# fc1 of a macaron block as seven half-size products (one level of Strassen's scheme) on one Trainium2 core

## What is computed

```python
x = x + 0.5 * ffn(layernorm(x))            # ffn: real(ifft(fft(x) @ w)) + bias, a 512 x 512 product M
x = x + attn(layernorm(x))
x = x + 0.5 * ffn(layernorm(x))
# attn(x):
h = layernorm(x) * norm1_w + norm1_b
x = x + causal_conv(h, K) + D * h          # K = mix @ exp(-tau dt t), per channel
g = layernorm(x) * norm2_w + norm2_b
g = gelu(g @ fc1_w.T + fc1_b)              # 512 -> 2048
g = g @ fc2_w.T + fc2_b                    # 2048 -> 512
return x + g
```

## Time and profile before

| | us |
|---|---|
| median of 3 runs (lowest to highest) | 2140.52 (2140.36 to 2143.08) |
| the profiled execution, its own time | 2143.72 |
| span of the profile | 2141.9 |
| PE busy | 1965.4 |
| DVE busy | 1247.0 |
| ACT busy | 748.8 |
| POOL busy | 537.4 |
| mean granted clock of TensorE | 0.969 of full |

### The profile page before, as it was taken

The page is one execution under the profiler, slowest core; times in us unless marked ns, Lnnn a source line. Parts: engine busy times, 40 slices in busy tenths (PEclk is TensorE's granted clock), DMA queues, the critical chain, the costliest instruction groups (busy, mean ns, idle before and its releaser), DMA issues.

```text
span 2141.9 us, 27911 instructions
## 1 busy us (share of the span) xinstructions
PE 1965.4 (92%) x10107; PEld 963.8 (45%) x10128; DVE 1247.0 (58%) x2099; ACT 748.8 (35%) x1003; POOL 537.4 (25%) x416
## 2 busy tenths in 40 slices
PE   7975877498859999999999999999999999999997
PEld 6432333276634444444444444444444444444443
DVE  4876999777955637274562727446282644628242
ACT  1365777664633314032230413223041322404111
POOL 0165777653421202021120201112020111202101
PEclk8997999799979999999999999999999999999998
DMA  7144332379781122131212213121222212122011
GB/s 246 79 174 160 118 118 98 94 199 311 229 250 40 40 59 58 62 79 36 64 40 59 60 60 78 40 59 40 60 60 64 74 40 59 40 59 60 25 35 40
DMA packets 231288, 191.02 MB, mean 89 GB/s; under 512 B 142594, under 2 KB 176898, under 8 KB 230403
## 3 DMA queue, kind: packets, MB, share of 16 engines
q1 hardware_dynamic: 231172, 189.34, 30.4%
HBM read 100.69 MB, written 63.41 MB: 77 GB/s over the span
## 4 chain that ended last, share of the span: by engine, by line
PE 78%; DVE 7%; DMA 5%; issue 5%; POOL 2%; ACT 2%; SPq 1%; ACTq 0%; DVEq 0%; POOLq 0%; another core or an unknown queue 0%
PE psum L1555 31%; PE psum L1572 31%; PE psum L1459 9%; DMA arena<-in_x 3%; PE psum L1510 2%; PE psum L1501 1%; PE psum L1422 1%; DVE ring L1189 1%; DVE arena L1133 1%; DVE bn L966 1%; DVE bn L1141 1%; PE psum L1519 1%; PE psum L1433 1%; PE psum L1440 1%; DVE taps L1089 1%
## 5 line engine op out<-in xcount | busy, mean ns | idle before, releaser
L1555 PE MATMUL psum<-arena 128*128 128x512 f16 x3072 | 668.6, 380 | 25.1 <-DMA arena<-taps 24.7
L1572 PE MATMUL psum<-arena 128*128 128x512 f16 x3072 | 665.7, 379 | 0.0
L846 ACT ACTIVATE arena<-psum,b1p,sc 128x512 f32<-128x512 f32 x256 | 199.2, 778 | 1060.1 <-PE psum L1555 1059.0
L1555 PEld LDWEIGHTS psum<-arena 128*128 128x128 f16 x3072 | 300.7, 98 | 391.2 <-issue 31.8
L1572 PEld LDWEIGHTS psum<-arena 128*128 128x128 f16 x3072 | 300.5, 98 | 362.5
L565 POOL TENSOR_TENSOR va<-va,mhalf 128x4 f32<-128x4 f32 x80 | 91.0, 1141 | 1249.2 <-DVE va L959 1226.3
L1376 DVE SCALAR_TENSOR_TENSOR arena<-psum,sc,arena 128x512 f32<-128x512 f32 x64 | 48.0, 751 | 578.7 <-PE psum L1572 578.7
L1352 DVE SCALAR_TENSOR_TENSOR arena<-arena,sc 128x512 f16<-128x512 f32 x256 | 243.9, 953 | 9.1
L1459 PE MATMUL psum<-m_parts,taps 128*128 128x512 f16 x768 | 183.6, 390 | 69.5 <-DVE taps L1089 69.1
L1459 PE MATMUL psum<-m_parts,arena 128*128 128x512 f16 x768 | 170.8, 383 | 10.3 <-DMA arena<-taps 10.3
L1349 DVE TENSOR_SCALAR arena<-arena,sc 128x512 f16<-128x512 f32 x256 | 137.6, 537 | 51.1 <-ACT arena L846 50.8
(11 more groups left out here) (159 smaller groups left out, 1767.5 us busy)
## 6 DMA issues: line engine op xcount, KB each, us to landing
arena<-in_x SPq DMA_DIRECT2D x16, 1024.0 KB, 9.8
x_scratch<-arena SPq DMA_DIRECT2D x16, 1024.0 KB, 4.3
...
```

The source lines that it names most:

```text
L846: act.activation(h32[:, hc % 4, :], bank(hc % 2), ACT.Gelu, scale=scale(C_W1), bias=b1p[:, hc:hc + 1])\
L1555: last = pe.matmul(bank(hc % 2), w1_sb[:, a, k, hc * P:(hc + 1) * P], gt[:, b, k, :], start=(n == 0), stop=(n == 3 * KC - 1))
L1572: last = pe.matmul(bank(4 + j % 2), hid[:, a, hc, j * P:(j + 1) * P], w2_sb[:, b, hc, :], start=(n == 0), stop=(n == 3 * HC - 1))
```

## The change

The 2048 x 512 weight matrix is cut into blocks A11, A12, A21, A22 of 1024 hidden rows and 256 inputs, the 512 tokens of a group into two halves (tiles 0, 1 and tiles 2, 3). Seven products of 1024 x 256 by 256 x 256, for the combinations A11, A12, S1, S4, S3, N2, A22 of blocks (PROD = 7), take the place of eight. Per pair p of hidden chunks (HP = 8 pairs) each product is 2 (k) x 3 matmuls of 256 columns. Their sums are formed in three PSUM chains: chain a takes A11, then N2, S3 and A22, and is copied out by ACT after the first three (h_first, h_second, h_third); chain b holds A12; chain c S1, then S4. DVE adds them (c11, c22, c12) in `h32`, ACT takes Gelu there.

With it come: hid_high (the high part of the hidden activation) goes from DVE to POOL; z2 gets three more combinations (z2_mix) and is split and turned in two halves of three DMAs, through one buffer; z3_parts has two buffers for four tiles and the whole z3 stands in the PSUM banks 4 and 5; the second product stands behind step 4 of fc1 rather than behind fc1; mixed, residual and z2 of the next group stand behind fc1; each parity has one buffer for r and x2, so the load of r waits for the store of the output two groups before. In the preparation POOL mixes the scaled blocks (w1_mix), in two parts, the second during the first tiles of the first pass; ACT and DVE split them; the scratch holds 7 MB where it held 4, and 3 MB of it are loaded after the others. The scale of fc1's weights is 4 times lower.

```diff
+PROD = 7
+HB = HID // 2
+HP = HC // 2
+CB = C // 2
+TB = GT * P // 2
...
-        rbuf = [buffer(at4), buffer(at3)]
-        x2buf = [buffer(at3 + size), buffer(at3 + 2 * size)]
...
+        rbuf = [buffer(at2 + 3 * size), buffer(at4 + 2 * gt_cols + size)]
...
+        h32 = [ring[:, 0:2, :], ring[:, 2:4, :], spare[:, 2 * C:4 * C].rearrange("p (i c) -> p i c", i=2)]
+        z3_parts = spare[:, 0:2 * C].bitcast(F16).rearrange("p (j s c) -> p j s c", j=2, s=2)
+        z2_parts = taps_flat[:, 0:PROD * 2 * CB].rearrange("p (n s c) -> p n s c", n=PROD, s=2)
+        z3t = taps_flat[:, 2 * one_block:4 * one_block].rearrange("p (j s k t) -> p j s k t", j=GT, s=2, k=KC)
+        extra = psum[:, 6:8, :].rearrange("p a b -> p (a b)")[:, 0:3 * CB].rearrange("p (n c) -> p n c", n=3)
+        TURNS = ((0, 2), (2, 4), (4, 7))
...
+            def turn_z2(g, half):
+                for i, (a, b) in enumerate(TURNS):
+                    sp.wait_ge(z2_low, 6 * g + 3 * half + i + 1)
+                    sp.sem_inc(gate, 1)
+                    sp.dma_start_transpose(gt[:, 4 * a:4 * b, half * P:(half + 1) * P],
+                                           z2_parts[:, a:b, :, :].rearrange("p n s c -> p (n s c)"))\
+                      .then_inc(gt_turned[i], 16)
...
-                    sp.wait_ge(z2_low, 4 * g + 4)
+                    sp.wait_ge(z2_low, 6 * g + 6)
...
+                    sp.wait_ge(x3_ready, 4 * g)
+                    sp.dma_start(rows(out, g - 1), rbuf[1 - par]).then_inc(out_stored[1 - par], 16)
...
+                    if not is_first(g):
+                        sp.wait_ge(out_stored[1 - par], 16 * (pair + par))
+                    load_r(g + 1, 1 - par)
+                    sp.wait_ge(product[S4], HP * g + HP)
+                    sp.sem_inc(gate, 1)
+                    for half in range(2):
+                        turn_z2(g + 1, half)
...
+            def w1_mix(k):
+                pool.wait_ge(w1_scaled, 4 * k + 4)
+                a22, a21, a11, a12 = [scaled[k][:, i, :] for i in range(4)]
+                pool.tensor_tensor(a22, a21, a22, ALU.add).then_inc(w1_mixed, 1)
+                pool.tensor_tensor(a21, a11, a21, ALU.subtract).then_inc(w1_mixed, 1)
+                pool.wait_ge(w1_mixed, 4 * k + 2)
+                pool.tensor_tensor(a11, a11, a22, ALU.subtract).then_inc(w1_mixed, 1)
+                pool.wait_ge(w1_mixed, 4 * k + 3)
+                pool.tensor_tensor(a12, a12, a11, ALU.add).then_inc(w1_mixed, 1)
...
+            def hid_high(g, p, lower):
+                ready = (h22_ready, h1_ready)[lower]
+                pool.wait_ge(ready, HP * g + p + 1)
+                if not lower:
+                    pool.wait_ge(h21_ready, HP * g + p + 1)
+                if p == 0 and not lower and not is_first(g):
+                    pool.wait_ge(fc2_psum, 4 * g)
+                pool.sem_inc(gate, 1)
+                pool.tensor_scalar(hid[:, 0, p if lower else HP + p, :], h32[p % 3][:, 0 if lower else 1, :],
+                                   scale(S_H), None, ALU.mult).then_inc(h_high, 1)
...
+                for p in range(HP):
+                    hid_high(g, p, False)
+                    hid_high(g, p, True)
+                    if not is_first(g) and p < 4:
+                        x2_biased(g - 1, p, 1 - par)
...
+                for s in range(HP + 1):
+                    p, n = s, HP * g + s + 1
+                    if s < HP:
+                        act.wait_ge(product[A11], n)
+                        if p >= 3:
+                            act.wait_ge(h_low, HC * g + 2 * p - 4)
+                        elif not is_first(g):
+                            act.wait_ge(h_low, HC * g)
+                        act.activation(h32[p % 3][:, 0, low], chain_a(p), ACT.Copy)\
+                           .then_inc(h_first, 1)
+                    if s > 0:
+                        q = s - 1
+                        act.wait_ge(product[S3], n - 1)
+                        act.activation(h32[q % 3][:, 1, high], chain_a(q), ACT.Copy)\
+                           .then_inc(h_third, 1)
+                        if not is_first(g) and s <= 4:
+                            z3_norm(g - 1, 1 - par, s - 1)
+                    if s < HP:
+                        act.wait_ge(product[N2], n)
+                        act.activation(h32[p % 3][:, 0, high], chain_a(p), ACT.Copy)\
+                           .then_inc(h_second, 1)
+                    if s > 0:
+                        act.wait_ge(c22_sum, n - 1)
+                        gelu(g, q, False, high, h32[q % 3][:, 1, high], h22_ready)
+                        act.wait_ge(product[A22], n - 1)
+                        gelu(g, q, False, low, chain_a(q), h21_ready)
+                        act.wait_ge(c12_sum, n - 1)
+                        gelu(g, q, True, whole, h32[q % 3][:, 0, whole], h1_ready)
+                if not is_last(g):
+                    z2_all(g + 1)
...
+            def z2_mix(g, half):
...
+                dve.tensor_tensor(extra[:, 0, :], second[:, 1, :], second[:, 0, :], ALU.subtract)\
+                   .then_inc(z2_mixed, 1)
+                dve.tensor_tensor(second[:, 0, :], second[:, 0, :], first[:, 0, :], ALU.subtract)\
+                   .then_inc(z2_mixed, 1)
+                dve.tensor_tensor(extra[:, 1, :], second[:, 0, :], second[:, 1, :], ALU.subtract)\
+                   .then_inc(z2_mixed, 1)
+                dve.tensor_tensor(extra[:, 2, :], first[:, 1, :], extra[:, 1, :], ALU.add).then_inc(z2_mixed, 1)
...
+            def z3_whole(g, j, par):
+                if j >= 2 or not is_first(g):
+                    dve.wait_ge(z3_low, 4 * g + j - 1 if j >= 2 else 4 * g)
+                dve.tensor_scalar(bank(4 + j % 2), rbuf[par][:, j, :], va[:, 4, j:j + 1], va[:, 5, j:j + 1],
+                                  ALU.mult, ALU.add).then_inc(z3_ready, 1)
...
+                for s in range(HP + 1):
+                    if s > 0:
+                        c22(g, s - 1)
+                    if s > 1:
+                        hid_low(g, s - 2, False)
+                    if s < HP:
+                        c11(g, s)
+                    if not is_first(g) and s < 4:
+                        z3_whole(g - 1, s, 1 - par)
+                    if s > 0:
+                        c12(g, s - 1)
+                    if s > 1:
+                        hid_low(g, s - 2, True)
+                    if not is_first(g) and 1 <= s < 5:
+                        z3_split(g - 1, s - 1)
+                    if not is_first(g) and s == 4:
+                        for j in range(GT):
+                            x3(g - 1, j, 1 - par)
+                hid_low(g, HP - 1, False)
+                hid_low(g, HP - 1, True)
+                if not is_last(g):
                     for j in range(GT):
+                        mixed(g + 1, j, pair + par, 1 - par)
+                    mixed_shift(g + 1)
+                    for j in range(GT):
+                        residual(g + 1, j, 1 - par)
+                x2(g, 0, par)
+                if not is_last(g):
+                    z2_mix(g + 1, 0)
+                    z2_split(g + 1, 0)
+                    z2_mix(g + 1, 1)
+                x2(g, 1, par)
+                if not is_last(g):
+                    z2_split(g + 1, 1)
+                x2(g, 2, par)
+                x2(g, 3, par)
...
-                pe.wait_ge(z3t_turned[j], 16 * (g + 1))
-                if not (is_first(g) and j < 2):
+                pe.wait_ge(z3t_turned[j % 2], 16 * (2 * g + j // 2 + 1))
+                if j == 0:
+                    pe.wait_ge(z3_low, 4 * g + 4)
+                if j >= 2:
                     pe.wait_ge(x3_ready, 4 * g + j - 1)
-                ffn(bank(6 + j % 2), z3t[:, j, :, :, :], ffn2_psum)
-            pe.wait_ge(w1_loaded, 16 * 8)
...
+            def part_product(i, p, chain, start, stop):
+                n = 0
+                for k in range(2):
+                    for a, b in PASSES:
+                        last = pe.matmul(chain(p),
+                                         w1_sb[i][:, a, k, p * P:(p + 1) * P], gt[:, 4 * i + 2 * b + k, :],
+                                         start=start and n == 0, stop=stop and n == 5, skip_group_check=True)
+                        n += 1
+                last.then_inc(product[i], 1)
+            def p1(g, p):
+                if not (is_first(g) and p < 2):
+                    pe.wait_ge(h21_ready, HP * g + p - 1)
+                part_product(A11, p, chain_a, True, False)
+            def p2(g, p):
+                if not (is_first(g) and p < 2):
+                    pe.wait_ge(c11_sum, HP * g + p - 1)
+                part_product(A12, p, chain_b, True, True)
+            def p6(g, p):
+                pe.wait_ge(h_first, HP * g + p + 1)
+                part_product(N2, p, chain_a, False, False)
+            def p5(g, p):
+                if not (is_first(g) and p < 2):
+                    pe.wait_ge(c12_sum, HP * g + p - 1)
```

(40 more changed lines are left out.)

497 lines of the change are left out of this document (290 added, 207 removed).

## The result

| | us |
|---|---|
| before, median of 20 runs beside the changed kernel | 2143.12 |
| changed kernel, median of 20 runs (lowest to highest) | 2137.82 (2134.06 to 2140.07) |
| ratio, with its 95% interval | 0.9976 (0.9969 to 0.9983) |
| profiled execution, and its span | 2136.47, 2134.5 |

What follows compares the result with a forecast made beforehand. TensorE was taken to bound the kernel, without a gap from 630 us on. Terms -76.0 + 6.4 + 34.5 + 12 + 8 + 1.5 = -13.6 us gave 2126.9 us against the 2140.52 median; range 2097 to 2168.

Steps and rivals of the forecast that it cites:

- What fc1 saves: TensorE's fc1: 336 matmuls of 256 columns at 0.1092 us, 4.75 us less per group, -76.0 us for 16.
- The rival that weight loads show: fc1: weight loads show at 256 columns, 0.141 us per matmul, +172, kernel 2299 us; chance 0.03.
- The three chains: Inside fc1's steps: TensorE waits for other engines' copies and sums, 0.4 us per group, +6.4 us.
- The wait ahead of the second product: After fc1's step 4: TensorE waits for DVE's last z3_split, 2.3 us in each of 15 groups, +34.5 us (24 to 45).
- the floor: Second product's wait at least 1.6 us, against 2.0 taken; part of the everything-at-its-floor rival, 2102 us, chance 0.27.
- the rival's threshold of 0.82 us: Last stage: the price per hid_high on POOL from about which the port-fills rival decides.
- the rival: Last stage, the port fills: hid_high near 1.4 us overfills the POOL and DVE port, kernel 2174 us; chance 0.18.
- Its term of 16 us for the other steps: Port-fills rival, steps without x2_biased: 0.2 us over in each, 5 per group, +16 us.
- fc2's window: Work moved behind fc1 fits under fc2, covered by 1.2 us, at nothing; missed-window rival 2147 us, chance 0.10.
- First fc1: Before the first fc1: longer TensorE wait from serial turns, sums, copies and 3 MB more weights, +8 us (5 to 14).
- Tail: Kernel's end: tiles 2 and 3 wait for the turns of 0 and 1, +1.5 us (1 to 3).
- Preparation: Kernel's front: M's peak reduced near 81 us, +8, and mixings in the first tiles, +4; together +12 us (5 to 18).

Runs made afterwards that it cites:

- experiment 9: Changed kernel with VectorE's split of the last z3 tile put ahead of the c12 sum and low part in each group's fifth step: 2114.66 us.
- experiment 4: Changed kernel with GpSimd's four low parts of the mixed weight blocks moved two tiles later, away from VectorE's bias split: 2131.48 us.
- experiment 1: Changed kernel with the first 2 MB copy of the convolution's taps issued ahead of the waits for the four mixed weight blocks: 2117.48 us.
- experiment 2: Changed kernel with the first two copies of the taps issued ahead of the waits for the mixed weight blocks: 2111.21 us.
- experiment 3: Changed kernel with the making of the four mixed weight blocks left out and plain blocks stored in their places: 2113.11 us.

## Why the prediction was wrong

By its own steps:

- **What fc1 saves**, -76.0: right. Matmuls of 256 columns follow each other at 0.1092 us, as worked out, also without a gap over a whole group (experiment 9). The rival that weight loads show is out.
- **The three chains**, +6.4: they cost nothing. With the second product's wait removed, a group is 0.07 us longer than its matmuls. Only the very first fc1 stops once, 0.9 us.
- **The wait ahead of the second product**, +34.5: right place, right cause, and the floor instead of the middle: 1.72 us a group, 25.8 in all. The low part that I took to be slowed took 0.74 us at 857.55. Two of the terms were wrong in opposite ways: hid_high is 1.58 us and not 0.95, but as a one-input operation it slows VectorE far less than the 1.64 for 0.75 us of the earlier trace rows. Beside it a low part takes 1.10 us (852.96 in the changed kernel). The assumption that the port is held for the length of GpSimd's operation failed for this one-input operation (that low part ends some 0.3 us before the hid_high that began at 852.84), and with it the rival's threshold of 0.82 us: the price was twice that and the rival did not come. Its term of 16 us for the other steps did not follow from its own numbers either: 2 x 1.4 + 1.5 is 4.3 us, less than the 4.587 of a step. The Trainium skill (GPSIMD Engine Reference, section 3.1) has 769 ns for a best-case loop over 512 elements; the measured operation took twice that.
- **fc2's window**, at nothing: right. No wait of TensorE stands in fc2.
- **The turns of the loop**, not in the sum: +7.7, five times 1.1 to 1.8 us. I had read x2_shift's wait at the head of a group as no different from before, which left VectorE 0.7 us of room for c22 of pair 0; at a turn it starts later than that.
- **First fc1**, +8: 9.1. **Tail**, +1.5: 1.4. Right.
- So the last stage is -76.0 + 25.8 + 7.7 + 1.4 + 0.9 = -40.2 by these. Most of the 3.3 us to the measured -43.5 are the kernel before's own: its first fc1 ran 2.9 us over (44.47 for 41.60, with a mean granted clock of 0.71 of full in its first 10 us) against 1.5 in the changed one, and its periods are on average 93.32 and not 93.24 (1.1 us in fourteen). That is 2.5; the last 0.8 us stay open.
- **Preparation**, +12 (5 to 18): this is the step that failed, with +26.3. Its first half came as said: the peak of M is reduced at 81.06 where 72.92 stood in the earlier trace rows, +8.1. The later mixings were to cost 4 and cost 7.2, since a two-input run of GpSimd slows three steps of VectorE's bias split from 1.5 us in all to 7.1 (experiment 4: 6.3 us); the forecast had put the delay down to ScalarE's waiting. And 12.2 us were not in it at all. It named the mixing's operations on POOL, ACT and DVE, and never asked what stands behind the four new stores in SyncE's queue: the bias row, a copy of 2 MB, and the load that the tiles wait for. By this accounting experiment 1 should give 12.2 plus 6.5 for the copy taken out of the way, 18.7, and gave 18.4; experiment 2 25.2, and gave 24.7. That the whole 26.3 come from the mixing is shown (experiment 3), and so is that the front follows the moment of the first copy (the table); the split into 15.3 and 12.2 is read from the trace, and these two sums are what supports it.

The last stage was 10 us better than counted and the front 14 us worse, the first fc1 and the convolution 2 us worse: together the 6 us (on the spans) between forecast and result. The range held the time. That the forecast came within 6 us of it is luck: two errors of 10 and 14 us nearly cancelled.
